# In projection weights laid out by DMA transposes instead of TensorE transposes, in a macaron block with a state-space middle

## The reference

```python
x = x + 0.5 * ffn(layernorm(x), w_gate, w_up, w_down)
x = x + ssm(layernorm(x), ...)
x = x + 0.5 * ffn(layernorm(x), w_gate, w_up, w_down)

def ffn(x, wg, wu, wd):            # integer weights, times 1/127; hidden size 768
    return (silu(x @ wg.T) * (x @ wu.T)) @ wd.T

def ssm(x, ...):                   # inner size 512, state size 128
    x_in, z = split(x @ in_proj_w.T, 2)           # in_proj_w is (1024, 256)
    xc = causal_conv_4_taps(x_in) + conv_b
    dt_r, Bm, _ = split(xc @ x_proj_w.T, [16, 144])
    delta = clip(softplus(dt_r @ dt_proj_w.T + dt_proj_b), 0.001, 0.1)
    A = -exp(A_log)
    A_bar = exp(delta * A);  B_bar = (A_bar - 1) / A * Bm
    h[t] = A_bar[t] * h[t-1] + B_bar[t]           # over 2048 steps
    y = h @ C_proj_w.T + xc * D
    return (y * silu(z)) @ out_proj_w.T
```

## Time and profile before

| | us |
|---|---|
| median of 3 runs | 510.67 (510.43 to 512.41) |
| the profiled execution | 513.12 |
| its span, first to last instruction | 511.3 |
| TensorE busy | 486.6 (95%) |
| VectorE busy | 382.5 (75%) |
| ScalarE busy | 310.5 (61%) |
| GpSimd busy | 233.3 (46%) |

### The profile page before, as it was taken

One profiled execution on the slowest core, in us unless ns is written; L12 is line 12 of the kernel. 1 busy time (PEld: TensorE's weight loads), 2 busy tenths in 40 slices (PEclk: granted clock), 3 DMA queues, 4 the chain that ended last, 5 costly groups with the idle time before them and its releaser, 6 DMA issues. The chain is left out here.

```text
span 511.3 us, 7826 instructions
## 1 busy us (share of the span) xinstructions
PE 486.6 (95%) x2643; PEld 285.3 (56%) x2643; DVE 382.5 (75%) x799; ACT 310.5 (61%) x540; POOL 233.3 (46%) x220
## 2 busy tenths in 40 slices
PE   3878999989999999999999999999999999999996
PEld 2446435634576465745484466646484557634865
DVE  4889987796867877696968887696968594868462
ACT  5384864376746876386746865587729763567042
POOL 1242156327281628346562828254652736154233
PEclk9899999989999999999999999999999999999999
DMA  8700000041015300730044201520052002100101
GB/s 285 212 4 3 2 0 3 0 112 15 1 24 144 42 3 9 126 74 3 2 82 85 43 3 22 144 43 3 3 116 40 12 1 33 52 2 0 44 1 44
DMA packets 53818, 23.44 MB, mean 46 GB/s; under 512 B 41728, under 2 KB 52992, under 8 KB 53760
## 3 DMA queue, kind: packets, MB, share of 16 engines
q1 hardware_dynamic: 52944, 21.84, 19.2%
q10 hardware_dynamic: 816, 0.79, 0.5%
HBM read 8.99 MB, written 4.19 MB: 26 GB/s over the span
## 5 line engine op out<-in xcount | busy, mean ns | idle before, releaser
L498 POOL TENSOR_TENSOR hl<-h,hh 128x512 f16<-128x512 f32 x90 | 110.2, 1237 | 98.3 <-ACT hh L727 97.8
L1122 DVE SCALAR_TENSOR_TENSOR xc<-xi,cw,xc 128x512 f32<-128x512 f32 x96 | 80.4, 847 | 7.9 <-ACT xi L745 7.3
L1100 DVE SCALAR_TENSOR_TENSOR h<-sg,hsm,q 128x512 f32<-128x512 f32 x90 | 66.1, 741 | 14.6 <-POOL hl L498 8.1
L515 POOL TENSOR_TENSOR xcl<-xc,xch 128x512 f16<-128x512 f32 x32 | 41.5, 1305 | 61.5 <-ACT xch L752 61.5
L719 ACT ACTIVATE sg<-q 128x512 f32<-128x512 f32 x90 | 53.1, 592 | 25.1 <-PE q L1755 22.0
L727 ACT ACTIVATE hh<-h 128x512 f16<-128x512 f32 x90 | 55.6, 627 | 19.9 <-DVE h L1100 18.4
L1108 DVE SCALAR_TENSOR_TENSOR x<-dp,x 128x512 f32<-128x512 f32 x48 | 33.1, 689 | 41.5 <-PE dp L1755 41.4
L1755 PE MATMUL q<-xt_Bnext,wih 128*128 128x512 f16 x224 | 59.2, 379 | 0.3 <-DVE xt_Bnext L1056 0.2
L1755 PE MATMUL dp<-wo,yu 128*128 128x256 f32 x256 | 56.7, 379 | 0.0
L1755 PE MATMUL dp<-wd,hh 128*128 128x256 bf16 x384 | 52.7, 273 | 1.5 <-ACT hh L727 1.0
L1755 PE MATMUL dp<-wd,hl 128*128 128x256 bf16 x384 | 52.7, 273 | 0.6 <-issue 0.6
(11 more groups left out here) (203 smaller groups left out, 797.9 us busy)
## 6 DMA issues: line engine op xcount, KB each, us to landing
x<-in_L_attn_x_dram SPq DMA_DIRECT2D x8, 512.0 KB, 4.4
out_dram<-x SPq DMA_DIRECT2D x16, 256.0 KB, 2.5
xc<-in_L_attn_in_proj_w_dram SPq DMA_DIRECT2D x1, 1024.0 KB, 11.2
hl<-in_L_ffn_w_up_dram ACTq DMA_DIRECT2D x3, 256.0 KB, 6.3
hh<-in_L_ffn_w_gate_dram SPq DMA_DIRECT2D x3, 256.0 KB, 7.0
hh<-in_L_ffn_w_down_dram SPq DMA_DIRECT2D x1, 768.0 KB, 8.4
yu<-n_L_attn_out_proj_w_dram SPq DMA_DIRECT2D x1, 512.0 KB, 5.5
yu<-in_L_attn_x_proj_w_dram SPq DMA_DIRECT2D x1, 256.0 KB, 11.8
```

What stands on the lines that cost most here:

```text
L498: pool.tensor_tensor(HL[g.hid(k)][:, c, :], H[:, j, :], HH[g.hid(k)][:, c, :], ALU.subtract)\
L515: pool.tensor_tensor(XCL[:, m, :], XC[g.b][:, m, :], XCH[:, m, :], ALU.subtract)\
L1100: dve.scalar_tensor_tensor(out=H[:, first % 3, :], in0=SG[:, first % 2, :], scalar=HSM[:, c:c + 1], in1=q[bank][:, :], op0=ALU.mult, op1=A ...
L1122: dve.scalar_tensor_tensor(out=XC[s][:, m, :], in0=XI[s][:, m, k:k + TILE], scalar=CW[:, m, k:k + 1], in1=XC[s][:, m, :], op0=ALU.mult, op ...
```

## The change

The four fills i0 to i3 leave FIRST, and with them the 16 TensorE transposes, the four copies by ScalarE and the four subtractions by VectorE. Instead ScalarE scales the rows in place and casts four blocks of rows at a time to 16 bits (`in_proj_high`), GpSimd subtracts (`in_proj_low`), both in the natural layout, and SP transposes the high and the low parts of x and z by four DMAs into WIH and WIL, whose layout changes accordingly. `in_proj` of `Half(0)` waits for them. The first down products get an explicit wait for the down weights, which the fills gave them before. The seven steps of the decay's series move from VectorE to GpSimd. The remaining edits reorder: the statistics of half 1's tile on VectorE, a few steps of ScalarE and VectorE in the start and in the last two halves, and two pairs of TensorE steps in FINAL.

```diff
--- before.py
+++ after.py
...
-         ("up5", "A", -1), ("fill", "d1", -1), ("fill", "d2", -1), ("bound", "", -1), ("fill", "i0", -1),
-         ("dtn", "", -1), ("count1", "", -1), ("fill", "i2", -1), ("fill", "i1", -1), ("fill", "i3", -1),
+         ("up5", "A", -1), ("fill", "d1", -1), ("fill", "d2", -1), ("bound", "", -1), ("dtn", "", -1),
+         ("count1", "", -1), ("flag1", "", -1), ("more1", "", -1), ("down00", "A", -1), ("down01", "A", -1),
...
-FINAL = (("ix0", "B", 7), ("ix1", "B", 7), ("iz0", "B", 7), ("ix2", "B", 7), ("iz1", "B", 7), ("ix3", "B", 7),
+FINAL = (("ix0", "B", 7), ("ix1", "B", 7), ("ix2", "B", 7), ("iz0", "B", 7), ("iz1", "B", 7), ("ix3", "B", 7),
...
-         ("gate4", "C", 7), ("up4", "C", 7), ("gate5", "C", 7), ("up5", "C", 7), ("cp0", "B", 7), ("cp1", "B", 7),
+         ("gate4", "C", 7), ("up4", "C", 7), ("gate5", "C", 7), ("cp0", "B", 7), ("up5", "C", 7), ("cp1", "B", 7),
...
-        WIH = sb("wih", [P, KD, 2 * INNER], F16)
-        WIL = sb("wil", [P, KD, 2 * INNER], F16)
+        WIH = sb("wih", [P, 2 * IC, KD, P], F16)
+        WIL = sb("wil", [P, 2 * IC, KD, P], F16)
...
-        NIS = XC[1][:, :, :].rearrange("p c (u f) -> p (c u) f", f=D)
+        NIH, NIL = (XC[1][:, 2 * n:2 * n + 2, :].bitcast(F16).rearrange("p c (u f) -> p (c u) f", f=D) for n in range(2))
...
+            def turn_in_proj(part):
+
+                rows = slice(IC * part, IC * (part + 1))
+                for ready, natural, turned_to in ((in_high, NIH, WIH), (in_low, NIL, WIL)):
+                    sp.wait_ge(ready, part + 1)
+                    sp.dma_start_transpose(turned_to[:, rows, :, :].rearrange("p c k t -> p (c k) t"),
+                                           natural[:, rows, :].rearrange("p c f -> p (c f)")).then_inc(in_turned[part], 16)
+
             load(Half(1))
+            turn_in_proj(0)
+            turn_in_proj(1)
             turn(Half(1), "A")
...
+            rates = [0]
+
+            def step_on(ins):
+
+                rates[0] += 1
+                ins.then_inc(rate_step, 1)
+                pool.wait_ge(rate_step, rates[0])
+
+            def decay_series():
+
+                pool.wait_ge(rate_begun, 1)
+                step_on(pool.tensor_scalar(EY[:, :], ER[:, :], 1.0 / 5040, 1.0 / 720, ALU.mult, ALU.add))
+                for term in (120, 24, 6, 2, 1):
+                    step_on(pool.tensor_scalar(EY[:, :], EY[:, :], ER[:, 0:1], 1.0 / term, ALU.mult, ALU.add))
+                pool.tensor_scalar(EY[:, :], EY[:, :], ER[:, 0:1], 1.0, ALU.mult, ALU.add).then_inc(rate_ready, 1)
+
+            def in_proj_low(part):
+
+                rows = slice(IC * part, IC * (part + 1))
+                pool.wait_ge(in_high, part + 1)
+                pool.tensor_tensor(NIL[:, rows, :], NI[:, rows, :], NIH[:, rows, :], ALU.subtract).then_inc(in_low, 1)
...
-            hidden_low(before, "A", (0, 1, 2, 3, 4, 5))
+            hidden_low(before, "A", (0, 1, 2))
+            in_proj_low(0)
+            hidden_low(before, "A", (3, 4))
+            in_proj_low(1)
+            hidden_low(before, "A", (5,))
             root(before, "Bnext", 0)
             root(before, "Bnext", 1)
+            decay_series()
             conv_low(start, (0, 1, 2, 3))
...
-                act.activation(NIS[:, c, :], NI[:, c, :], ACT.Copy, scale=RSC[:, c:c + 1]).then_inc(in_scaled, 1)
+                act.activation(NI[:, c, :], NI[:, c, :], ACT.Copy, scale=RSC[:, c:c + 1]).then_inc(in_scaled, 1)
+
+            def in_proj_high(part):
+
+                rows = slice(IC * part, IC * (part + 1))
+                act.wait_ge(in_scaled, IC * (part + 1))
+                act.activation(NIH[:, rows, :], NI[:, rows, :], ACT.Copy).then_inc(in_high, 1)
...
             scale_row(2)
             scale_row(3)
-            scale_row(4)
-            norm_hi(start, "A", (1,))
-            fill("d0")
             hidden_high(before, "A", (2, 3))
             gate(before, "A", (5,))
+            in_proj_high(0)
+            norm_hi(start, "A", (1,))
+            scale_row(4)
+            fill("d0")
             fill("d1")
             scale_row(5)
             scale_row(6)
             fill("d2")
             hidden_high(before, "A", (4,))
             scale_row(7)
-            fill("i0")
+            in_proj_high(1)
             copy_rank()
-            fill("i2")
             hidden_high(before, "A", (5,))
-            fill("i1")
             scale_x(0)
             scale_x(1)
-            fill("i3")
             gate(start, "A", (0, 1))
...
             conv_begin(late, (3,))
+            conv_high(late, (0,))
             norm_hi(late, "C", (0, 1))
             silu_z(late, (2,))
             conv_in(late, (3,))
-            conv_high(late, (0,))
             silu_z(late, (3,))
-            conv_high(late, (1, 2))
-            gate(late, "C", (0, 1))
+            conv_high(late, (1,))
+            gate(late, "C", (0,))
+            conv_high(late, (2,))
+            gate(late, "C", (1,))
             hidden_high(late, "C", (0,))
             act.preload_act_table_set("natural_log_exp_and_others")
...
+                dve.scalar_tensor_tensor(out=ER[:, :], in0=EK[:, :], scalar=2.12194440e-4, in1=ER[:, :],
+                                               op0=ALU.mult, op1=ALU.add).then_inc(rate_begun, 1)
...
+                dve.wait_ge(rate_ready, 1)
...
-            halo(start)
+            stats(first, "A", (0, 1, 2, 3))
+            variance_tile(first, "A")
             residual(start, "A", 0)
             stats(start, "Bnext", (0, 1))
+            halo(start)
             skip_y(start, (3,))
...
             stats(first, "C", (0, 1))
-            stats(first, "A", (0, 1, 2, 3))
-            variance_tile(first, "A")
             variance(first, "C", (0,))
...
-            normalize(late, "C", (0,))
+            normalize(late, "C", (0, 1))
             conv(late, 0, (2,))
-            normalize(late, "C", (1,))
             conv(late, 0, (1,))
             normalize(late, "C", (2,))
             conv(late, 0, (0,))
+            normalize(late, "C", (3,))
             conv(late, 1, (2,))
-            normalize(late, "C", (3,))
...
-            normalize(last, "C", (2,))
             norm_lo_half(last, 0)
             hidden_half(last, 0, (0,))
+            normalize(last, "C", (2,))
...
-                    pe.matmul(tp[1][:, :], WIH[:, 0, 0:P], WIH[:, 0, 0:TILE], start=True, stop=True)
+                    pe.matmul(tp[1][:, :], WIH[:, 0, 0, :], WIH[:, 0:2, :, :], start=True, stop=True)
...
+                if g.h == 0 and m == 0:
+                    pe.wait_ge(in_turned[z], 32)
                 product(g, what, "B",
-                        [(w[:, kc, col], XT["Bnext"][:, low, :, kc, :] if dma else (XL if low else XH)[g.b][:, kc, :])
+                        [(w[:, IC * z + m, kc, :], XT["Bnext"][:, low, :, kc, :] if dma else (XL if low else XH)[g.b][:, kc, :])
...
+                if g.h < 0:
+                    pe.wait_ge(w_act, HC + HC // 2)
...
```

More of the change, by code:

```diff
@@ L154, in plan @@
         elif what == "fill":
-            last = "w_dve" if part[:-1] in ("i", "x", "t") else "w_act"
+            last = "w_dve" if part[:-1] in ("x", "t") else "w_act"
             count[last] += 1
@@ L359, in macaron @@
         parts_full, parts_read, parts_step = sem("parts_full"), sem("parts_read"), sem("parts_step")
-        rows_ready, in_scaled = sem("rows_ready"), sem("in_scaled")
+        rows_ready, in_scaled, in_high, in_low = (
+            sem(n) for n in ("rows_ready", "in_scaled", "in_high", "in_low"))
+        in_turned = [sem(f"in_turned{n}") for n in range(2)]
+        rate_begun, rate_step, rate_ready = (sem(n) for n in ("rate_begun", "rate_step", "rate_ready"))
         w_hi = sem("w_hi")
@@ L627, in fill @@
                                    scale=HSI[:, 2 * j + 1:2 * j + 2]).then_inc(w_act, 1)
-                elif w == "i":
-                    act.activation(WIH[:, j // 2, 512 * (j % 2):512 * (j % 2 + 1)], bank[:, :], ACT.Copy)\
-                        .then_inc(w_hi, 1)
                 elif w == "x":
@@ L907, in _ @@
             hidden_high(start, "A", (0,))
-            silu_z(start, (1,))
             conv_high(start, (2,))
-            silu_z(start, (2,))
+            silu_z(start, (1, 2))
             conv_high(start, (3,))
@@ L981, in _ @@
             gate_half(last, 1, (1,))
+            gate_half(last, 1, (2,))
             hidden_high_half(last, 1, (0,))
+            gate_half(last, 1, (3,))
             hidden_high_half(last, 1, (1,))
-            gate_half(last, 1, (2,))
-            gate_half(last, 1, (3,))
             hidden_high_half(last, 1, (2,))
@@ L1281, in decay_rate @@
                                                op0=ALU.mult, op1=ALU.add))
-                chain(dve.scalar_tensor_tensor(out=ER[:, :], in0=EK[:, :], scalar=2.12194440e-4, in1=ER[:, :],
-                                               op0=ALU.mult, op1=ALU.add))
-            def decay_series():
```

(14 more changed lines are left out.)

12 lines of the change are left out of this document (removed), and 15 rows, old and new, of the table FIRST.

## The result

| | before | after |
|---|---|---|
| median, us | 510.74 (9 runs, 510.43 to 512.41) | 513.12 (9 runs, 512.20 to 513.89) |
| ratio | | 1.0037 (95%: 1.0026 to 1.0048) |
| profiled execution, us | 513.12 | 512.93 |
| its span, us | 511.3 | 511.1 |

The change makes the kernel 2.4 us slower, 0.37%. That is inside the band of 0.5% to which I gave 0.60, but 3.0 us above the forecast of 510.1 and just outside its range (to 512.9). The two profiled executions took the same time, but the one of before is 2.4 us above its own median and the one of after is at its median; so the traces are compared by stages that both share, not by their ends.

A forecast was written before the change was run, and what follows sets the result against it. TensorE bounds the kernel, so only its waits in three places count: from 510.67 us, +2.7 (set-up), -2.8 (first full half) and -0.5 (last tiles) gave 510.1 us; own range 508.9 to 511.6, wider range 506.6 to 512.9.

The forecast's parts named there:

- set-up: chunk 5 in GpSimd's queue: Set-up: chunk 5's low part waits behind GpSimd's long subtraction, making the second residual add 1.7 us late.
- set-up: the clock: Set-up: TensorE's emptier stretch brings a half-clock dip of some 3 us from about 43 us, costing 1.6 us.
- VectorE's credit, up to add 4: Before the in projection: one removed VectorE subtraction lies behind the new wait and gives back 0.6 us.
- first full half: At 98 to 112 us: statistics moved ahead remove waits before the up product, gaining 2.8 us.
- last tiles: From 455 us: earlier high parts shorten TensorE's 0.61 us wait for GpSimd's low part, gaining 0.5 us.
- ScalarE, GpSimd, the wait of the down product: Set-up: casts 1.05 us, long subtraction 2.3, chunk 5's low part ends at 42.95, first down product at 43.0.
- the split's own wait shrinks: First full half: ScalarE's split at 110.15 waits less than 1.62 us, because VectorE's chain is 1.87 us early too.
- the other swaps: Last half and stand-in matmuls' operands: remaining reorders keep counts and shapes, so 0 us.
- Base: The profiled 513.12 us contains one clock dip, at 112 us; the median without it is 510.67 us.
- 4: Set-up from 43 us: clock stays low, the dip lasting twice as long; 511.7 us, chance 0.12.
- Rival 5: First full half: the wait stays because another releaser takes the root's place; 512.9 us, chance 0.08.
- Rival 1: Set-up holds: chunk 5's low part is in time and the clock stays; 507.4 us, chance 0.21.

The follow-up runs named there:

- f1: The changed kernel run again, unchanged: 513.11 us, ratio to the kernel before 1.0041.
- e2: Changed kernel plus twelve matmuls that nobody reads, in TensorE's set-up gap: 511.83 us, ratio to the kernel before 1.001.
- e3: Changed kernel with chunk 5's low part (GpSimd) and high part (ScalarE) ahead of the in projection's second parts, plus twelve gap matmuls: 508.12 us, ratio 0.9933.
- e9: Changed kernel with chunk 5's parts ahead of the in projection's second parts on GpSimd and ScalarE, no added matmuls: 510.21 us, ratio to before 0.9985.
- e1: Changed kernel with chunk 5's low part ahead of the in projection's second low part on GpSimd alone: 510.23 us, ratio to before 0.9973.
- e5: e3 with the statistics of half 1's tile put back to their old place: 509.67 us, ratio to the kernel before 0.9964.
- e7: e3 with mean and variance of half 1's tile computed behind the variance of the tile before: 508.21 us, ratio to the kernel before 0.9929.
- e4: Kernel before with only the statistics of half 1's tile moved ahead and the halo copy behind its statistics: 509.69 us, ratio 0.9972.
- e6: Kernel before with only the reorders of the last two halves: 511.65 us, ratio 1.0003.
- e0: The kernel before, unchanged, one more profiled execution: 512.72 us.
- e8: e7 with both in projection casts and low parts behind chunk 5's on ScalarE and GpSimd, eight gap matmuls instead of twelve: 515.31 us, ratio 1.0094.

## Why the prediction was wrong

The terms of its sum, as the ledger and the runs measure them (where there are two figures: the first profile of the changed kernel, f1):

| term | forecast, us | measured, us |
|---|---|---|
| set-up: chunk 5 in GpSimd's queue | +1.7 | +2.1 (e2 against e3) |
| set-up: the clock | +1.6 | +1.8, +2.6 (up5 to add 1 against e2) |
| VectorE's credit, up to add 4 | -0.6 | -0.1 |
| first full half | -2.8 | -2.0 |
| last tiles | -0.5 | -0.1 |
| sum | -0.6 | +1.7, +2.5 (+2.4 by the medians) |

The direction of every term was right, and every size was off to the slower side. The steps that failed are thus five sizes and not one. The largest miss that both traces show is the first full half (0.8 us); the clock missed by 0.2 in one trace and by 1.0 in the other.

1. **ScalarE, GpSimd, the wait of the down product: right.** The casts took 1.05 us (forecast 1.05), the long subtraction 2.13 (2.3), chunk 5's low part ended at 42.80 (42.95) and the first down product's last matmul ran at 43.10. The delay that this makes was 2.1 us, not 1.7. What starts the first down product I had wrong, as had the profile: the flag (e9), which the change did not delay. The DMA transposes and the decay's series cost nothing, as forecast (e1, e5).
2. **The clock: "I take 1.6, between 0 (no dip) and 3.2 (two such)".** The dip came, but not of that form: half clock not for some 3 us from about 43, but for about 10 (37 to 47 and 38 to 48), the first of it in the gap, where it costs nothing. I had let TensorE run through "with TensorE busy throughout", as in the dips of the earlier trace rows; but its down product stops again for chunk 5's low part, and while it did, the clock stayed low. e1 and e9 take that stop away, and their half clock is a third shorter (7 us).
3. **"1.7 - 0.6": the credit of VectorE.** The removed subtractions and series are worth 0.9 us behind the set-up (e5, e7), and at 55 us the changed kernel shows 0.7 of it (add 1 is 3.7 us late, the in projection 3.0, each against the profile before). But the moved statistics lose it again at 89 us, beside GpSimd's gate product, where the forecast put nothing: add 1 to add 4 is 0.8 us longer with them alone (e4), 0.9 shorter with the set-up alone (e5) and 0.1 shorter with both (47.74 against 47.80). The loss hangs on the instant. In e2, with the order of the changed kernel, the same step stands beside the same gate products, takes 0.16 us, and add 1 to add 4 is 46.97:

```profile
87.49 0.16 DVE L1075 TENSOR_SCALAR ve_A<-mv_A 128x4 f32<-128x4 f32 x1
```

4. **The first full half, "I take 2.8".** Measured 2.0, next to the lower figure that I had named and passed over (1.9). The normalization came 1.87 us early, as forecast. The step that failed is "the split's own wait shrinks": it shrank from 1.62 us only to 0.90, and 0.56 of TensorE's wait stayed with it. The step that it waits for took 0.40 us at the same place before; in the changed kernel it falls together with a subtraction on GpSimd (VectorE, then GpSimd):

```profile
110.36 1.29 DVE L1088 TENSOR_SCALAR xn<-x,mv_C,rs_C 128x256 f32<-128x256 f32 x1
```

```profile
110.34 1.16 POOL L549 TENSOR_TENSOR xcl<-xc,xch 128x512 f16<-128x512 f32 x1 [2.43 <-ACT xch L794]
```

That collision is not new. In the kernel before, a subtraction on GpSimd (108.09 to 109.25) falls on the two steps ahead, which take 1.0 us more than in the changed kernel (1.53 at 108.91):

```profile
107.26 2.53 DVE L1122 SCALAR_TENSOR_TENSOR xc<-xi,cw,xc 128x512 f32<-128x512 f32 x2
```

The 10.36 us that I took from the next half as the time without waits do not hold here. This is read from the traces; no run takes the collision away.

5. **The last tiles, 0.5.** The first wait went, but only 0.25 us came of it, and one of "the other swaps", which I had put at 0, took 0.2 of that back (e6).
6. **Base: right.** I read the 513.12 of the profiled execution as 510.7 and one dip. The dip is 1.8 us of that; another 0.5 is that up5 starts at 31.20, where it starts at 30.71 in e6. e0 shows another execution with the dip elsewhere and about the same time.

No rival came as written. Nearest is 4 (the clock stays low for longer), but its half clock was to begin at 43 us and not in the gap. Rival 5 has nearly the measured time (512.9), but not the mechanism: 1.40 of the 1.96 us went. Rival 1, the set-up holds at 507.4, is 0.7 under what the repaired kernels reach (508.1 to 508.2).

## What to carry to other kernels

When a queue gets a long instruction, look for the short one behind it on which the busiest engine waits (one step moved by one place was worth 2.9 us here). Look at the waits before pricing a lower clock: in these runs the half clock lasted 10 us where TensorE stopped a second time within it and 7 where it did not. Work moved to an idle stretch of VectorE may cost more there if GpSimd is in the middle of long instructions. And when a sum misses by more than any one term can explain, measure every term in a run of its own: here all five were off. Where a branch on a loaded value stands ahead of a start, hold that start against the value's write in several kernels before believing the releaser that a profile names.

## What the runs showed of the hardware

Small VectorE steps of 128x4 or 128x16, some 0.2 us by themselves, could last until GpSimd's running instruction ended: 1.31 us in the changed kernel, up to 2.17 in e8, with ends that fall on GpSimd's. They did not always: the step that takes 1.31 us in six traces with that order (after, f1, e1, e9, e3, e4) took 0.16 in e2. The Trainium skill has a rule that fits in SBUF — State Buffer, Who interferes with whom: in its two-port modes VectorE contends with GpSimd, and whoever issues first has the shared ports for the whole instruction; a VectorE instruction with two inputs from SBUF contends with one of GpSimd that reads SBUF. The traces agree, in the 1.31 as in the 0.16 us; in which mode these steps ran they do not show.

TensorE's half clock came and went between executions of the same kernel (e0 at 40 to 44 us, the profile of before at 112 to 115). With the gap of 3.3 us in the set-up it came in all four traces taken (after, f1, e1, e9), with the sixteen transposes in its place in one of five (e0), with the twelve added matmuls in three of four (e2, e3, e7; not e5), over by 40 us. In e8, with eight of them and then a standstill of 7.2 us, it came at 41 us. In e2 the clock was at 0.50 before the first added matmul, and in e1 from 35 us on, when the gap had only begun; so the gap's length alone is not the cause. The Trainium skill, TensorE: Matmul & The Clock Gate, Part 4 (PE-mode transpose), says that transposes do not count as a busy TensorE in the same way as other matmuls; the traces here do not bear that out, though they do not test it by itself. What sets off the half clock in a single execution stays open.
